# Second attention of an early-fusion network: the order of GpSimd's reciprocal roots and additions in one loop

## The chip, the cores and the metric

The kernel runs on one core of one Trainium2 chip. The time is that of the device, in microseconds (us), from the start of the one launch to its end. Each core has a matrix engine (TensorE, PE in the profile, with its weight loads as PEld), a vector engine (VectorE, DVE), a scalar engine (ScalarE, ACT), GpSimd (POOL) and a queue that issues transfers (SyncE, SP). Each engine works through its own list of instructions in order; semaphores are what one engine waits for on another.

## The reference, cut to what matters

The network has four levels. Each level adds an attention and then a feed-forward layer to `h` (16 batches of 192 tokens, 192 values each), and each of the eight layers works on normed rows of `h`:

```python
h = h + L0_attn(layernorm(h)); h = h + L0_ffn(layernorm(h))
h = h + L1_attn(layernorm(h)); h = h + L1_ffn(layernorm(h))
...

def _L1_attn_ref(x, Wqkv, Wproj, bproj, s_q, s_k, s_v, s_attn, s_after):
    qkv = x @ Wqkv.T                      # 12 heads of 16
    q = fake_quant(q, s_q, -4, 3) * scale; k, v likewise
    attn = fake_quant((q @ k.T) / N, s_attn, 0, 7)     # no softmax
    out = fake_quant(attn @ v, s_after, -4, 3)
    return out @ Wproj.T + bproj
```

The change lies in the second attention, `L1_attn`. The layer behind it is a mixture of 16 experts, whose router needs the rows of `h + L1_attn(...)` normed once more and multiplied by a router matrix; that is done in the same loop. Both norms need `1 / sqrt(variance + eps)` of each row, which is called the root here.

## The kernel before, in words

The program is a row of stages. `attention1` is the stage of the second attention; it stands behind the first mixture of experts and ahead of the routing of the second. It goes over the 16 batches. A batch is 192 rows of `h`, held as two halves of 96 partitions, so a `[96, 384]` tile is a batch's `h`.

The five engines each have a loop over `n`, written out pass by pass, in which the steps of several batches are interleaved: in pass `n` the scores of batch `n` are made, while batch `n+1` is turned and projected, batch `n+2` is collected and its norm taken, and batch `n-1` is projected out. What ties the loops together are the semaphores in `S`.

A batch's way through the loops, with the lines of the profile:

- VectorE: `collect_part` (L1545) adds the weighted expert answers to `h`. `spread_of(0, n)` (L1556, L1559, L1561) takes mean and variance of the incoming rows and signals `var0`. `norm_in` (L1570) waits for `root0` and writes `rows`. This is done for batch `n+2` in pass `n`, with `spread_in(n + 2)` behind `take_scores(n, 3)` and `norm_in(n + 2)` ahead of `take_scores(n, 5)`.
- TensorE: `turn_in` transposes `rows` (L207, `t_bank`), `queries` and `keys` (L1330) and `values` (L927, `t_bank`) project them in f32; `scores` (L1356) and `weigh` (L1369) are small bf16 matmuls; `project_out` (L927, `b_bank<-a_wp,a_o`) makes the attention's output. `turn_normed` (L207, `b_bank`) and `route_scores` (L927, `b_bank<-a_router`) serve the router.
- ScalarE copies and scales what TensorE leaves in PSUM (L1446, L1453, L1460, L1476), and writes the second norm's rows `rows2` (`norm_out`, L1485).
- VectorE clips to the quantized range (L1538, L1603), adds the projected output to `h` (`add`, L1613), takes its mean and variance with `spread_of(1, n)` (`var1`), and, once `root1` is there, the shift of the second norm (`shift_of`, L1581).
- GpSimd does four things: `add_bias(n)` (L1302) adds the projection's bias to `h` once the rows of batch `n` are normed; `grow(n)` (L1307) adds `rows2` to `h` once ScalarE wrote them; `root_of(0, n)` and `root_of(1, n)` (L1289) raise the variance to the power -0.5 for the incoming and for the finished rows. It issues no transfers in this stage.

SyncE brings the expert answers of batches ahead (waits for `collected`) and stores the finished normed rows (waits for `rows2`).

The order of each engine's list is written by hand. No planner and no priorities are in it: GpSimd takes the next step only when the one before it has had its semaphore.

Of the kernel before, what the change touches and what calls it, by code (L numbers as in the profile page):

```python
# [21 lines left out]
B, N, D = 16, 192, 192  # L22
# [1186 lines left out]
def attention1(k, weights, answers, wts, logits, normed, E):  # L1209
# [8 lines left out]
    with ExitStack() as ctx:  # L1218
# [41 lines left out]
        @block.sync  # L1260
        def _(sp):
            def bring(m):
                if m >= AHEAD:
                    sp.wait_ge(S["collected"], m - AHEAD + 1)
                for r in range(2):
                    sp.dma_start(got[m % AHEAD][:, r], answers[r * T + m * N:r * T + m * N + N].rearrange("(t p) d -> p t d", p=H2)
                                 ).then_inc(got_in[m % AHEAD], 16)

            def store(n):
                to = normed[n * N:(n + 1) * N].rearrange("(t p) d -> p t d", p=H2)  # L1270
                sp.wait_ge(S["rows2"], n + 1)
                sp.dma_start(to[:, :, 0:D], rows2[n % KEPT][:]).then_inc(kept[n % KEPT], 16)
                sp.dma_start(to[:, :, D:WIDE], rows2[n % KEPT][:, :, 128:D]).then_inc(kept[n % KEPT], 16)

            for m in range(6):
                bring(m)
            for n in range(B + 1):
                if n + 6 < B:
                    bring(n + 6)
                if n >= 1:  # L1280
                    store(n - 1)
            for u in range(KEPT):
                sp.wait_ge(kept[u], 32 * (B // KEPT))

        @block.gpsimd
        def _(pool):
            def root_of(r, n):
                pool.wait_ge(S[f"var{r}"], n + 1)
                nc.gpsimd.tensor_tensor(root[r][:], var[r][:], half[:], ALU.pow).then_inc(S[f"root{r}"], 1)  # L1289

            nc.gpsimd.memset(half[:], -0.5).then_inc(S["preset"], 1)
            for u in range(2):
                nc.gpsimd.memset(v[u][:], 0.0).then_inc(S["preset"], 1)
            pool.wait_ge(S["preset"], 3)
            root_of(0, 0)
            root_of(0, 1)
            pool.wait_ge(weights.loaded, weights.LOADED)

            def add_bias(n):
                pool.wait_ge(S["rows"], n + 1)  # L1300
                hb = h[:, 2 * n:2 * n + 2, :]
                nc.gpsimd.tensor_tensor(hb, hb, bias[:].unsqueeze(1).broadcast_to([H2, 2, D]), ALU.add).then_inc(S["biased"], 1)  # L1302

            def grow(n):
                pool.wait_ge(S["rows2"], n + 1)
                hb = h[:, 2 * n:2 * n + 2, :]
                nc.gpsimd.tensor_tensor(hb, hb, rows2[n % KEPT][:], ALU.add).then_inc(S["grown"], 1)  # L1307

            add_bias(0)
            for n in range(B + 2):  # L1310
                if n + 1 < B:
                    add_bias(n + 1)
                if 2 <= n:
                    grow(n - 2)
                if 1 <= n <= B:
                    root_of(1, n - 1)
                if n + 2 < B:
                    root_of(0, n + 2)

        @block.tensor  # L1320
        def _(pe):
# [1816 lines left out]
```

## Time and profile before

| | before |
|---|---|
| runs, median (lowest to highest) | 2682.95 us (2680.21 to 2687.97), 3 runs |
| profiled execution, its own time | 2685.28 us |
| its span in the trace | 2683.2 us |
| TensorE busy | 2387.4 us, 89% of the span |
| VectorE, ScalarE, GpSimd busy | 49%, 32%, 18% of the span |
| mean granted TensorE clock | 0.898 |
| GpSimd in this stage, first and last root | 602.9 and 873.4 us from the span's start |

The profile's times count from the span's start. The stage of the change takes some 280 of the 2683 us. The granted clock is the share of full TensorE speed (2.4 GHz) in a stretch: 1.00 and 0.50 are the two levels, and a value between them is a stretch that has some of both. "Idle before, with a releaser" is the time in which an engine had nothing to do and what ended it. Matmul ends are modelled.

### The profile page before, as it was taken

The page shows a single profiled execution, that of the slowest core. Times are in us where ns is not written, and L with a number is a line of the kernel's source. Part 1 is how long each engine was busy: PE and PEld are TensorE (multiplying, and loading weights), DVE is VectorE, ACT ScalarE, POOL GpSimd, SP SyncE. Part 2 cuts the span into 40 slices and gives each one's busy share as a digit, 9 for nine tenths or more (in the row PEclk, how much of TensorE's full clock was granted, in tenths as well). Part 3 has the DMA queues.
Part 4 walks back from the last instruction along what each step waited for, and adds up shares of the span by engine and source line. Part 5 has one row for each costly group of instructions (what it writes and reads, how often), then busy time and mean ns, then how long its engine had stood idle before and what let it go on. Part 6 is the DMA issues. An engine that isn't in the chain of part 4 may idle for free. (4 is left out here: it accounts for less than half of the span.)

```text
span 2683.2 us, 52183 instructions
## 1 busy us (share of the span) xinstructions
PE 2387.4 (89%) x17933; PEld 2084.2 (78%) x17933; DVE 1326.3 (49%) x3861; ACT 871.1 (32%) x2122; POOL 490.1 (18%) x583
## 2 busy tenths in 40 slices
PE   8968999988999489997999766999978899999997
PEld 8958999977777388887788665878747788888886
DVE  2663333326665711112688744555567456372644
ACT  2411222215555033332232212343444333343431
POOL 1233322222222334443122101000011000010100
PEclk8979999988655689998999856999989999999999
DMA  3134464511100368673000001000001452726355
GB/s 110 28 84 134 136 173 145 161 43 32 30 22 16 96 190 239 206 223 110 18 18 9 1 1 28 8 7 9 7 12 33 144 137 66 204 54 171 91 150 156
DMA packets 234529, 234.76 MB, mean 87 GB/s; under 512 B 29736, under 2 KB 214942, under 8 KB 234270
## 3 DMA queue, kind: packets, MB, share of 16 engines
q1 hardware_dynamic: 220638, 203.56, 27.4%
q0 software_dynamic: 11520, 27.54, 3.3%
q10 hardware_dynamic: 2240, 1.99, 0.3%
q8 instruction: 73, 1.20, 0.2%
q14 instruction: 58, 0.48, 0.1%
HBM read 277.77 MB, written 35.45 MB: 117 GB/s over the span
## 5 line engine op out<-in xcount | busy, mean ns | idle before, releaser
L732 PE MATMUL f_pg<-f_vxT,f_w 128*128 128x128 f32 x2112 | 261.0, 278 | 3.1 <-DVE f_vxT L802 3.1
L732 PEld LDWEIGHTS f_pg<-f_vxT,f_w 128*128 128x128 f32 x2112 | 253.4, 194 | 7.2 <-DVE f_vxT L802 4.6
L744 PE MATMUL f_po<-f_wd,f_hid 128*128 128x192 f32 x1440 | 254.3, 326 | 1.2 <-DVE f_vout L828 0.7
L744 PEld LDWEIGHTS f_po<-f_wd,f_hid 128*128 128x128 f32 x1440 | 231.2, 190 | 2.0 <-issue 1.7
L705 POOL DMA_INDIRECT f_answers<-f_vout,f_to_row x120 | 118.8, 990 | 423.9 <-DVE f_vout L826 250.7
L813 DVE TENSOR_TENSOR f_hid<-f_silu,f_pg 128x128 f32<-128x128 f32 x336 | 81.9, 285 | 214.8 <-ACT f_silu L781 199.5
L781 ACT ACTIVATE f_silu<-f_pg 128x128 f32<-128x128 f32 x336 | 78.4, 277 | 293.0 <-PE f_pg L738 274.0
L786 ACT ACTIVATE f_hid<-f_pg,f_b 128x128 f32<-128x128 f32 x384 | 110.9, 370 | 192.8 <-issue 109.0
L802 DVE COPY f_vxT<-f_pt 128x256 f32<-128x256 f32 x120 | 50.6, 422 | 208.1 <-PE f_pt L724 206.0
L738 PE MATMUL f_pg<-f_vxT,f_wr 64*128 64x128 f32 x2112 | 151.3, 285 | 0.0
L1926 DVE TENSOR_REDUCE a_low<-a_s_bank 96x6 f32<-96x1152 f32 x64 | 86.6, 1354 | 116.2 <-PE a_s_bank L1781 115.8
L738 PEld LDWEIGHTS f_pg<-f_vxT,f_wr 64*128 64x128 f32 x2112 | 128.2, 189 | 14.7 <-issue 0.4
L2767 PE MATMUL s_bank<-s_w,s_arena 128*128 128x192 f32 x768 | 133.4, 330 | 4.8 <-DMA s_b<-s_b_of 4.8
L2587 POOL TENSOR_TENSOR s_small<-s_small,s_half 128x2 f32<-128x2 f32 x64 | 44.4, 694 | 508.4 <-DVE s_small L2914 508.4
L2767 PEld LDWEIGHTS s_bank<-s_w,s_arena 128*128 128x128 f32 x768 | 123.9, 190 | 15.2 <-issue 9.3
L2984 DVE TENSOR_TENSOR s_y<-s_bank,s_b 128x384 f32<-128x384 f32 x64 | 35.3, 557 | 201.5 <-PE s_bank L2767 173.0
L2861 ACT ACTIVATE s_arena<-s_bank,s_b 128x256 f32<-128x256 f32 x192 | 73.6, 482 | 165.9 <-PE s_bank L2753 165.9
L699 POOL DMA_INDIRECT f_vrows<-f_normed,f_from_row x120 | 117.1, 976 | 43.2 <-issue 35.6
L2671 PE MATMUL s_bank<-h,s_arena 96*128 96x192 f32 x512 | 99.3, 337 | 22.2 <-ACT s_arena L2830 21.5
L2694 PE MATMUL s_bank<-s_ys,s_combine 128*96 128x193 f32 x512 | 97.0, 339 | 15.8 <-DMA s_ys<-s_y 9.5
L2671 PEld LDWEIGHTS s_bank<-h,s_arena 96*128 96x128 f32 x512 | 83.2, 191 | 34.5 <-ACT s_arena L2830 34.0
L2813 ACT ACTIVATE s_arena<-s_bank,s_small 128x192 f32<-128x192 f32 x128 | 52.7, 417 | 168.0 <-DVE s_combine L2897 168.0
(398 smaller groups left out, 4889.7 us busy)
## 6 DMA issues: line engine op xcount, KB each, us to landing
f_wd<-in_L_ffn_W SPq DMA_DIRECT2D x64, 576.0 KB
f_wd<-in_L_ffn_WdT SPq DMA_DIRECT2D x56, 576.0 KB
f_w<-in_L_ffn_W SPq DMA_DIRECT2D x64, 384.0 KB
f_w<-in_L_ffn_WgT SPq DMA_DIRECT2D x56, 384.0 KB
f_w<-in_L_ffn_WuT SPq DMA_DIRECT2D x56, 384.0 KB
s_w<-in_w SPq DMA_DIRECT2D x64, 288.0 KB, 3.7
f_wr<-in_L_ffn_W SPq DMA_DIRECT2D x128, 96.0 KB
s_w<-in_w SPq DMA_DIRECT2D x64, 192.0 KB, 4.3
```

What stands on the lines that cost most here:

```text
L699: pool.indirect_dma_start(out=rows[n % 3][:], out_offset=None, in_=normed, in_offset=bass.IndirectOffsetOnAxis(ap=from_row[:, n:n + 1], ax ...
L705: pool.indirect_dma_start(out=answers, out_offset=bass.IndirectOffsetOnAxis(ap=to_row[:, n:n + 1], axis=0), in_=out[n % 3][:], in_offset=N ...
L732: pe.matmul(pg[j][:, a * ROWS:(a + 1) * ROWS], lift[a][r][:, j * 128:j * 128 + 128], xT[r][:, 0, :], start=(a == 0), stop=False, skip_grou ...
L738: last = pe.matmul(pg[i + s * HALF][:, a * ROWS:(a + 1) * ROWS], rest[a][r][of, i * 128:i * 128 + 128], xT[r][of, 1, :], start=False, stop ...
L744: last = pe.matmul(po[:, 0:D], hid[r][:, j, :], wd[r][:, j, :], start=(at == 0), stop=(at == FC - 1))
L781: nc.scalar.activation(silu[at % 2][:], pg[j][:, 0:ROWS], ACT.Silu).then_inc(gates, 1)
L786: nc.scalar.activation(hid[r][:, j, :], pg[j][:, 0:ROWS], ACT.Gelu, bias=bias[:, ds(e, 1), j:j + 1].rearrange("p o n -> p (o n)")).then_in ...
L813: nc.vector.tensor_tensor(hid[r][:, j, :], silu[at % 2][:], pg[j][:, ROWS:2 * ROWS], ALU.mult).then_inc(hidden, 1)
L1926: nc.vector.tensor_reduce(low[:, :, EACH * c:EACH * c + EACH, DH].rearrange("p t e -> p e t"), s_bank[0:H2, :, 0:2 * N].rearrange("p e (t ...
L2671: last = pe.matmul(split(2 + b % 2, D)[:, c, :], disp[b % 2][:, t, c * 128:c * 128 + 128], h[:, 2 * b + t, :], start=(t == 0), stop=(t == 1))
L2694: last = pe.matmul(split(6 + b % 2, XA, H2)[:, t, :], weights_of(g)[:, c, t * H2:t * H2 + H2], ys[g % FETCHED][:, c, :], start=(c == 0), s ...
L2767: last = pe.matmul(split(6 + s, D)[:, f, :], hid[2 * p + s][:, c, f * 128:f * 128 + 128], w2[2 * p + s][:, c, :], start=(c == 0), stop=(c ...
```

## The change

In GpSimd's loop of `attention1` the root of the incoming rows of batch `n + 2` is taken ahead of the addition of normed rows of batch `n - 2` and ahead of the root of the finished rows of batch `n - 1`. It stood behind both. The addition of the bias stays first in the pass. Nothing else is touched.

```diff
             for n in range(B + 2):
                 if n + 1 < B:
                     add_bias(n + 1)
+                if n + 2 < B:
+                    root_of(0, n + 2)
                 if 2 <= n:
                     grow(n - 2)
                 if 1 <= n <= B:
                     root_of(1, n - 1)
-                if n + 2 < B:
-                    root_of(0, n + 2)
```

## Rows read from the trace of the kernel before

**Rows 1.** The page: TensorE's granted clock in 40 slices, in tenths.

```profile
PEclk8979999988655689998999856999989999999999
```

**Rows 2.** Waits, 603 to 885 us: total, times, longest.

```profile
DVE a_rows L1570 <- POOL a_root L1289: 20.9, 14, 1.5
...
PE a_t_bank L207 <- DVE a_rows L1570: 16.2, 8, 2.5
```

**Rows 3.** Timeline of a pass: start, duration, engine, line, idle before.

```profile
729.25 0.17 DVE L1561 TENSOR_SCALAR a_var<-a_mv 96x2 f32<-96x2 f32 x1
...
730.78 0.99 POOL L1307 TENSOR_TENSOR h<-h,a_rows 96x384 f32<-96x384 f32 x1 [10.12 <-ACT a_rows L1485]
...
731.54 0.61 DVE L1613 SCALAR_TENSOR_TENSOR h<-a_b_bank,a_s,h 96x384 f32<-96x384 f32 x1 [1.32 <-PE a_b_bank L927]
...
734.16 0.17 DVE L1561 TENSOR_SCALAR a_var<-a_mv 96x2 f32<-96x2 f32 x1
...
734.26 0.36 PE L1356 MATMUL a_s_bank<-a_qs,a_ks 32*96 32x192 bf16 x4
...
734.41 1.36 POOL L1289 TENSOR_TENSOR a_root<-a_var,a_half 96x2 f32<-96x2 f32 x2 [2.64 <-DVE a_var L1561]
...
735.88 0.67 DVE L1570 TENSOR_SCALAR a_rows<-h,a_mv,a_root 96x192 f32<-96x192 f32 x2 [1.55 <-POOL a_root L1289]
...
736.60 0.54 PE L207 MATMUL a_t_bank<-ident,a_rows 96*96 96x96 f32 x4 [1.97 <-DVE a_rows L1570]
736.62 1.53 POOL L1302 TENSOR_TENSOR h<-h,a_bias 96x384 f32<-96x384 f32 x1 [0.85 <-DVE a_rows L1570]
...
738.20 2.85 PE L1330 MATMUL a_p_bank<-a_xT,a_wqk 96*96 96x192 f32 x8
```

**Rows 4.** Timeline of the pass before it.

```profile
712.83 0.99 POOL L1307 TENSOR_TENSOR h<-h,a_rows 96x384 f32<-96x384 f32 x1 [8.81 <-ACT a_rows L1485]
...
718.39 0.67 DVE L1570 TENSOR_SCALAR a_rows<-h,a_mv,a_root 96x192 f32<-96x192 f32 x2 [1.55 <-POOL a_root L1289]
...
719.41 0.87 PE L207 MATMUL a_t_bank<-ident,a_rows 96*96 96x96 f32 x4
...
726.34 2.88 PE L1330 MATMUL a_p_bank<-a_xT,a_wqk 96*96 96x192 f32 x8
```

**Rows 5.** GpSimd's addition at the first, a middle and the last of 13 starts.

```profile
646.32 0.99 POOL L1307 TENSOR_TENSOR h<-h,a_rows 96x384 f32<-96x384 f32 x1 [9.59 <-ACT a_rows L1485]
...
746.99 0.99 POOL L1307 TENSOR_TENSOR h<-h,a_rows 96x384 f32<-96x384 f32 x1 [8.83 <-ACT a_rows L1485]
...
849.42 0.99 POOL L1307 TENSOR_TENSOR h<-h,a_rows 96x384 f32<-96x384 f32 x1 [8.84 <-ACT a_rows L1485]
```

**Rows 6.** Stretches: length, TensorE busy (instructions), granted clock, DMA share, GB/s.

```profile
731.00:732.00 1.00, 1.00 (x12) 0.96 0.39 101
...
737.00:738.00 1.00, 1.00 (x13) 0.96 0.00 0
...
765.00:766.00 1.00, 1.00 (x11) 0.89 0.25 62
```

**Rows 7.** Stretches: busy of PE, PEld, DVE, ACT, POOL, then the granted clock.

```profile
712.00:730.00 18.00, 18.00 (x98) 13.46 (x97) 10.51 (x31) 9.17 (x15) 3.88 (x4) 0.50 0.11 29
730.00:746.00 16.00, 14.03 (x97) 10.90 (x96) 10.24 (x30) 8.74 (x15) 3.88 (x4) 0.71 0.13 32
...
646.00:850.00 204.00, 190.22 (x1156) 145.30 (x1154) 122.80 (x351) 108.51 (x169) 46.92 (x49) 0.62 0.10 24
```

**Rows 8.** VectorE's shift of the second norm: shortest, median, longest ns.

```profile
L1581 DVE SCALAR_TENSOR_TENSOR a_shift<-a_mv,a_root x16: 149/972/975, 635.8 to 874.2; 96x2 f32<-96x2 f32 x16
```

**Rows 9.** Timeline near the stage's start, where the granted clock is 1.00.

```profile
623.03 0.36 PE L1356 MATMUL a_s_bank<-a_qs,a_ks 32*96 32x192 bf16 x4
...
624.92 1.47 PE L1330 MATMUL a_p_bank<-a_xT,a_wqk 96*96 96x192 f32 x8
...
632.35 0.36 PE L1356 MATMUL a_s_bank<-a_qs,a_ks 32*96 32x192 bf16 x4
```

## The prediction, made before the changed kernel ran

> **What bounds the kernel now.** I read the page first. TensorE is the busiest engine, and its granted clock dips in the middle of the first half of the span, in slices 11 to 14 [rows 1]; a slice is 67 us, so that dip, 671 to 939 us, is most of the stage of the second attention and the routing behind it. The waits of this stage came next [rows 2]: VectorE's norm of the incoming rows waits 14 times on GpSimd's root, 20.9 us in all, and TensorE's transposes of those rows wait 8 times on that norm, 16.2 us in all. 14 waits of VectorE but 8 of TensorE: in the other passes the stall is hidden. To see which, I read two successive passes in the timeline.
>
> In the first of them [rows 4] VectorE waits 1.55 us as well, yet its rows are ready at 719.06 and TensorE turns them at 719.41 with no idle time: TensorE is the bound, busy 18.00 us of 18.00 at half clock [rows 7]. In the second [rows 3], where TensorE is busy 14.03 of 16 us [rows 7], the granted clock is full from 731 to 738 us [rows 6]. TensorE comes through its list faster, stands 1.97 us for the rows, and turns them at 736.60. The stretch of full clock ends at 738, and the next begins at 765, so it comes in one pass of two here. GpSimd's addition marks the passes: 712.83, 730.78, 746.99 [rows 3 to 5]. So a pass all at half clock takes 17.95 us, one with a stretch of full clock 16.21, and the twelve passes from GpSimd's addition at 646.32 to that at 849.42 [rows 5] took 203.1 us, 16.9 each.
>
> **The change, part by part.** It adds and removes no instruction; 14 roots of the incoming rows move ahead of 12 additions and of 13 roots of the finished rows. No transfer is issued by GpSimd in the loop, and SyncE waits for nothing that GpSimd signals, so no queue but GpSimd's is reordered.
>
> *The moved root.* Its variance is ready at 729.42 (729.25 + 0.17) [rows 3]. GpSimd then has 10.12 us of idle time behind it and starts its addition only at 730.78. A root takes 0.68 us (two in 1.36) [rows 3]. After the change it runs from about 729.5 to 730.2, in time that was idle, 4 us before anyone asks for it. Cost: nothing; if the cover were gone, 0.7 us of the addition, for which nobody in the loop waits soon (ScalarE needs it four batches later).
>
> *What queues behind the new wait.* The addition waits for ScalarE's rows until 730.78, and the root of the finished rows needs its variance at 734.33 (734.16 + 0.17) [rows 3]. Both come later than 730.2, by 0.6 and 4.1 us. In this pass neither is held up.
>
> *The stall that goes.* VectorE's norm, in its place in VectorE's list, can start right after the finished rows' variance, at 734.33 and not at 735.88: 1.55 us earlier, its whole wait [rows 3]. The rows are there at 735.0. TensorE's scores end at 734.62, so it idles 0.4 us and not 1.97. What is late next is that same chain of the output projection, VectorE's addition and variance; its last 0.4 us remain as a wait for the rows.
>
> *Term 1.* Passes at half clock: 0, since TensorE is full there [rows 4, 7]. The 8 waits of TensorE [rows 2]: 8 x 1.55 = 12.4 us.
>
> *Term 2.* The transposes, the router scores and the query projection behind them move 1.55 us forward while the full clock ends, as before, at 738 [rows 3, 6]. The queries' 8 matmuls took 2.85 us at half clock, 0.356 us each [rows 3]; at full clock the same 8 took 1.47, or 0.184 each [rows 9]. They would start near 736.7 and have 1.2 us of full clock, six or seven matmuls, which saves 6.5 x 0.17 = 1.1 us in each such pass. A pass with a stretch then takes 16.21 - 1.55 - 1.1 = 13.6 us.
>
> *Term 3.* The stretches of full clock begin at 731 and 765 [rows 6], the first at the end of the unbroken row of key projection and output projection, 726.34 to about 731.5, when VectorE's addition gets its input (the longest piece of f32 matmuls in a pass) [rows 3, 4]; 765 is two passes on, and the same piece of the pass between raised nothing. Which pass gets one thus depends on the length of the passes, and that changes from 16.21 to 13.6 us. What share gets one afterwards the trace can't show. Bounds: one in two as now, or every one. I take 3 of 4, since a pass that follows at 13.6 us lies about 2.6 us earlier against the old rhythm and the unbroken piece is 5.2 us long. Over the twelve passes: 9 x 13.6 + 3 x 17.95 = 176.3, against 203.1: 26.8 us. With one in two it is 6 x 13.6 + 6 x 17.95 = 189.3, a gain of 13.8; with every one 163.2, a gain of 39.9. These sums hold terms 1 and 2 for the twelve passes; the first of the 8 waits lies ahead of them and adds 1.5.
>
> *The sum:* 26.8 + 1.5 = 28.3 us. The profiled execution took 2685.28 us, 2.1 us of it outside its span; that gives 2657.0, and set against the median of the runs shown, 2682.95, which is 2.3 lower, 2654.7. I forecast 2655 us.
>
> *A rule that speaks against the change.* VectorE's tiny shift, which stands near GpSimd's bias addition of 736.62 in time [rows 3], takes 0.97 us in the median and 0.15 at the shortest [rows 8]. So GpSimd work can hold up VectorE by 0.8 us. The moved root now runs from 729.5, and VectorE then is idle 1.32 us for TensorE, until 731.54 [rows 3]: up to that much is hidden. The Trainium skill says that GpSimd's SBUF interfaces are "shared with VectorE", with contention for instructions that use two ports or two SBUF inputs ("GPSIMD Engine Reference", section 1). By it the sum would be the same where VectorE idles, and the trace agrees.
>
> **The rivals.**
>
> *Only the wait goes.* The stretches become rarer or end sooner, or the passes fall out of the good rhythm half the time: the gain is term 1 alone up to the one-in-two case, 8 to 20 us, 2663 to 2675. For it: the rhythm of the stretches is strict now. Against: nothing takes term 2 away if the stretch keeps its length.
>
> *The full clock stays.* Near the stage's start the clock is full through, and a pass took 632.35 - 623.03 = 9.3 us [rows 9]; it lacked the router's scores and second transposes (an estimate: three times the 0.54 us of the four transposes at 736.60 [rows 3]), so a full pass would take about 10.9. What the rows show before the fall at 738 is the 1.97 us hole [rows 3, 6]; with 0.4 us left, the fall may not come. Twelve passes of 10.9 save 72 us: 2611. If it holds in six and the rest are as forecast (176.3 / 12 = 14.7), it is 203.1 - 6 x 10.9 - 6 x 14.7 = 49.5. Against: what TensorE does in that place is mostly transposes and small bf16 matmuls, and in the pass from 712 to 730 such work, without a gap, leaves the clock at 0.50 [rows 7]. The Trainium skill has a rule for this: activity releases the throttle, the default is the throttled state ("TensorE: Matmul & The Clock Gate", part 1). By it this rival is the outcome; the trace agrees only in that the fall follows a hole.
>
> *The wait is replaced.* The addition or the finished rows' root is held up by the new place, or VectorE is bound by its own work: no gain. Against: VectorE was busy 10.24 us of 16 in such a pass [rows 7], and the new place leaves 0.6 us of room. 2677 to 2691.
>
> *Slower: the stretches vanish.* If the new rhythm keeps missing the unbroken piece, every pass is one of 17.95 us: 12 x 17.95 = 215.4 against 203.1, 12 us more, 2695. A pass with a stretch and term 1 alone takes 14.66; it decides where fewer than one pass in three has one (17.95 - 3.3 x share = 16.9).
>
> **How the numbers follow.** The forecast case, gains of 20 to 42 us: 0.50. Only the wait goes: 0.21. The full clock stays in half of the passes or more, over 42 us: 0.17. The wait is replaced: 0.07. Slower: 0.05. 0.3% is 8 us, about what a measurement of this kernel can tell from no change. Faster by more than that: 0.88; within: 0.07; slower: 0.05. The range goes from 2632 (forecast case and the nearer third of the full-clock case) to 2673 (term 1 less a little), and leaves out 2 in 10.
>
> **What would show it.** VectorE's norm no longer waits on GpSimd's root (20.9 us to under 2). GpSimd's root of the incoming rows stands alone, some 4 us ahead of the other. TensorE's wait for the rows falls from 16.2 us to under 6. Passes alternate between about 13.6 and 17.95 us, and the granted clock of 646 to 850 us, 0.62 now [rows 7], rises to 0.67 or so. The other stages stay as they are. The prediction is wrong if the passes with a stretch stay above 15 us (term 2), if stretches come in half of the passes or fewer (term 3), or if they last longer than before (full clock).

## The result

The changed kernel takes 2603.12 us in the median of 4 runs (2595.94 to 2616.23), against 2681.58 us for the kernel before (4 runs, 2671.69 to 2687.97): a ratio of 0.9716, 95% interval 0.9662 to 0.9770. I forecast 2655 us and a range of 2632 to 2673; the time lies below both. The rival "The full clock stays" is what happened. The profiled execution took 2616.23 us, with a span of 2614.0; it is the slowest of the four.

The page of the changed kernel, its granted clock in 40 slices of 65 us, beside [rows 1]:

```profile
PEclk8979999998795999997999657999989999999999
```

Slices 11 to 14 stood at 6, 5, 5 and 6 [rows 1]. Now the half clock of the stage shows as the 8 and the 7 of slices 10 and 11 (588 to 719 us), and slice 12 is at 9; the 5 of slice 13 begins at 784 us and is mostly the routing behind the stage. To find the stage's end in each trace I took stretches with the same number of TensorE instructions. First the kernel before, a view that stands in none of its rows yet (columns as in [rows 7]; the clock is the third number from the end):

```profile
0.00:600.00 600.00, 545.45 (x4610) 518.48 (x4611) 239.74 (x958) 135.51 (x501) 157.34 (x193) 0.94 0.39 112
600.00:880.00 280.00, 257.09 (x1637) 199.69 (x1636) 165.85 (x480) 144.37 (x224) 61.47 (x64) 0.65 0.11 28
880.00:2683.20 1803.20, 1584.82 (x11688) 1366.08 (x11688) 920.73 (x2423) 591.20 (x1397) 271.34 (x326) 0.92 0.32 89
```

Then the changed kernel, with two stretches inside its stage at the end:

```profile
0.00:600.00 600.00, 545.55 (x4612) 520.57 (x4613) 239.73 (x959) 135.45 (x501) 157.49 (x193) 0.94 0.39 112
600.00:805.00 205.00, 192.72 (x1635) 153.07 (x1633) 158.87 (x480) 139.96 (x224) 63.15 (x64) 0.86 0.14 37
805.00:2614.00 1809.00, 1589.10 (x11688) 1367.50 (x11688) 920.75 (x2423) 586.70 (x1397) 271.21 (x326) 0.92 0.32 88
...
646.00:688.00 42.00, 42.00 (x227) 31.45 (x227) 24.67 (x74) 21.75 (x34) 7.68 (x9) 0.50 0.09 24
688.00:780.00 92.00, 88.83 (x867) 70.59 (x866) 85.78 (x261) 77.29 (x126) 36.27 (x36) 1.00 0.14 37
```

The stage with the same 64 GpSimd instructions went from 280 to 205 us and its mean clock from 0.65 to 0.86. The rest of the program gave 6 us back in this pair of executions (1809.0 against 1803.2), which leaves the 69 us between the two spans. That rest varies by more than this: from the stage's last addition to the end of the span it is 1794 us in the shortest and 1816 in the longest of the fourteen traces of this document, over the same code. So I give the length of the stage's passes beside the times below. Inside the stage there are now two regimes, and neither is the alternation that I forecast: a few passes at half clock, then full clock for 92 us on end.

The waits of the changed kernel from 603 to 885 us, beside [rows 2]:

```profile
DVE a_rows L1570 <- POOL a_root L1289: 0.8, 1, 0.8
...
PE a_t_bank L207 <- DVE a_rows L1570: 4.4, 11, 0.8
```

And its timeline in a pass at full clock, beside [rows 3]:

```profile
710.02 0.17 DVE L1561 TENSOR_SCALAR a_var<-a_mv 96x2 f32<-96x2 f32 x1
...
710.26 0.74 POOL L1289 TENSOR_TENSOR a_root<-a_var,a_half 96x2 f32<-96x2 f32 x1 [5.78 <-DVE a_var L1561]
...
710.98 1.32 POOL L1307 TENSOR_TENSOR h<-h,a_rows 96x384 f32<-96x384 f32 x1
...
712.29 0.17 DVE L1561 TENSOR_SCALAR a_var<-a_mv 96x2 f32<-96x2 f32 x1
...
712.37 0.67 DVE L1570 TENSOR_SCALAR a_rows<-h,a_mv,a_root 96x192 f32<-96x192 f32 x2
...
712.53 1.28 POOL L1289 TENSOR_TENSOR a_root<-a_var,a_half 96x2 f32<-96x2 f32 x1 [0.23 <-DVE a_var L1561]
...
713.09 0.54 PE L207 MATMUL a_t_bank<-ident,a_rows 96*96 96x96 f32 x4 [0.34 <-DVE a_rows L1570]
...
721.12 1.32 POOL L1307 TENSOR_TENSOR h<-h,a_rows 96x384 f32<-96x384 f32 x1
```

The root of the incoming rows now stands alone at 710.26, 2.1 us ahead of the norm at 712.37, which starts with no wait. TensorE's hole before its transposes (the idle time in front of them; this word from here on) is 0.34 us where it was 1.97 [rows 3]. From one addition to the next, 710.98 to 721.12, a pass takes 10.14 us. The fifteen passes from the first addition to the last take 12.2, 17.95, 17.95, 12.07, then eight of 9.16 to 10.24 (six of them 10.14), and 7.52 or less for the last three, which have less in them. With the two regimes read off, the same 17.95 us stands for half clock as before, so all of the gain is in how many passes run at full clock and in what such a pass takes.

### The profile page after: what moved, and what is told of

It reads as the page before. It is cut to its first block and busy times, and to the rows that moved or that the text cites. A ratio compares the mean times of both kernels' runs of the same rounds, so it can differ in the third digit from the quotient of the medians.

```text
span 2614.0 us, 52183 instructions
## 1 busy us (share of the span) xinstructions
PE 2327.4 (89%) x17933; PEld 2041.1 (78%) x17933; DVE 1319.4 (50%) x3861; ACT 862.1 (33%) x2122; POOL 491.8 (19%) x583
```

## The experiments

In each kernel the computation is the reference's. Some have *fillers* in front of TensorE's transposes of the incoming rows: matmuls of the identity with itself into unused columns of the same PSUM bank, work that nobody reads.

```diff
             def turn_in(n):
-                pe.wait_ge(S["rows"], n + 1)
                 pe.wait_ge(S["v8"], n)
+                if n >= 3:
+                    for _ in range(K):
+                        pe.matmul(t_bank[:, 384:512], k.ident[:], k.ident[:], start=True, stop=True)
+                pe.wait_ge(S["rows"], n + 1)
```

The fillers stand there from the fourth batch on. They fill the hole and, by the same act, give TensorE more work: what they show is that the hole with its lack of work matters, not which of the two. Ratios are to the kernel before on the same chip, whose median was 2683.1, 2681.8 and 2679.0 us in the three groups of runs; they are worked out from all runs, so they are not quite the quotients of the medians. What each of them did to the mean hole (TensorE's total wait for the rows by its count), to the twelve passes from GpSimd's first addition in the trace, and to the time:

| kernel | order of GpSimd's steps | mean hole, us | twelve passes, us | median us | ratio (95%) |
|---|---|---|---|---|---|
| before | addition, finished root, incoming root | 2.03 (8) | 203.1 | 2682 | 1 |
| half_hole | as after; norm waits for finished root | 1.30 (8) | 190.7 | 2676.57 | 0.9992 (0.9970 to 1.0014) |
| grow_first | addition, incoming, finished | 0.81 (10) | 167.5 | 2633.79 | 0.9818 (0.9778 to 0.9858) |
| grow_last | incoming, finished, addition | 0.38 (11) | 158.5 | 2636.32 | 0.9829 (0.9787 to 0.9872) |
| after | incoming, addition, finished | 0.40 (11) | 140.4 | 2603.12 | 0.9716 (0.9662 to 0.9770) |
| before_fill4 | before, 4 fillers | 1.43 (7) | 202.7 | 2673.31 | 0.9967 (0.9944 to 0.9990) |
| before_fill10 | before, 10 fillers | 0.37 (12) | 151.3 | 2616.11 | 0.9760 (0.9722 to 0.9797) |
| half_hole_fill4 | half_hole, 4 fillers | 0.40 (2) | 131.6 | 2600.11 | 0.9707 (0.9684 to 0.9729) |
| grow_first_fill4 | grow_first, 4 fillers | 0.2 (1) | 131.7 | 2593.76 | 0.9682 (0.9655 to 0.9708) |
| after_fill1 | after, 1 filler | 0.4 (1) | 120.8 | 2594.07 | 0.9664 (0.9645 to 0.9684) |

### Is it the clock? The old order with the hole filled

`before_fill10` is the kernel before with K = 10, nothing moved.

> The old order in GpSimd with ten filler matmuls ahead of the wait for the rows instead of four (2.7 us at full clock, 5.4 at half). With four, TensorE still stood 0.9 to 1.8 us for the rows and the clock still fell. Theory: the clock falls with the hole, and with the hole filled it stays at 1.00; a pass is then 10.14 + 1.55 for the root + 0.83 for VectorE's variance held up by GpSimd's addition = 12.5 us, and the kernel takes about 2683 - 13 x 4.4 + 5 = 2630 us. Rival, the clock follows something else: passes keep alternating, each low pass is 23 us long, and the kernel is slower than before, 2720 us or more.

Measured: 2616.11 us (2609.8 to 2623.56), ratio 0.9760. Its timeline in a pass, and a stretch of the stage:

```profile
706.34 0.99 POOL L1307 TENSOR_TENSOR h<-h,a_rows 96x384 f32<-96x384 f32 x1 [5.50 <-ACT a_rows L1488]
...
706.36 1.00 DVE L1564 TENSOR_SCALAR a_var<-a_mv 96x2 f32<-96x2 f32 x1
...
709.03 2.50 PE L1326 MATMUL a_t_bank<-ident 128*128 128x128 f32 x20
...
709.70 1.36 POOL L1289 TENSOR_TENSOR a_root<-a_var,a_half 96x2 f32<-96x2 f32 x2 [2.37 <-DVE a_var L1564]
...
711.17 0.67 DVE L1573 TENSOR_SCALAR a_rows<-h,a_mv,a_root 96x192 f32<-96x192 f32 x2 [1.55 <-POOL a_root L1289]
...
711.89 0.54 PE L207 MATMUL a_t_bank<-ident,a_rows 96*96 96x96 f32 x4 [0.36 <-DVE a_rows L1573]
```
```profile
646.00:790.00 144.00, 139.63 (x1322) 115.29 (x1319) 122.25 (x342) 98.25 (x158) 45.35 (x47) 1.00 0.13 32
```

VectorE still waits its whole 1.55 us; the wait that the change removes is untouched. Yet the clock is 1.00 through the stage and a pass takes 12.6 us, not 16.2 and 17.95. So some 66 of the change's 78 us can be had by keeping the clock alone. The timeline also gives the length of the hole without fillers: 2.50 + 0.36 = 2.86 us. It is longer than the 1.97 of [rows 3] since here VectorE's variance takes 1.00 us beside GpSimd's addition (706.34 and 706.36), where it took 0.17 at 729.25 [rows 3]. With 0.34 left in the changed kernel the difference is 2.5 us: 1.55 of the wait, 0.83 of that variance, and 0.1. That is the 12.60 - 10.14 = 2.46 us between the two full-clock passes.

Four fillers are too few for this order:

> The kernel before with the old order in GpSimd, plus filler: from the fourth batch on TensorE does four 128x128 f32 matmuls on the identity into unused columns of the bank of the transposes, ahead of its wait for the rows (about 1.0 us at full clock, 2.2 us at half clock). The stall of VectorE stays. Theory, the clock: the filler takes the place of the hole in TensorE's work, the granted clock stays at 1.00 for most passes, and a pass takes 10.14 + 1.55 = 11.7 us: 13 passes of about 5 us less, near 2620 us. Rival, the path: the stall is still on it and filler is only more work: no gain, or 10 us more, 2680 to 2695.

2673.31 us (10 runs, 2654.88 to 2686.22), ratio 0.9967 (0.9944 to 0.9990). TensorE in it, two passes:

```profile
766.72 1.16 PE L1326 MATMUL a_t_bank<-ident 128*128 128x128 f32 x8
...
768.76 0.54 PE L207 MATMUL a_t_bank<-ident,a_rows 96*96 96x96 f32 x4 [0.88 <-DVE a_rows L1573]
...
781.45 0.53 PE L207 MATMUL a_t_bank<-ident,a_rows 96*96 96x96 f32 x4 [1.79 <-DVE a_rows L1573]
```

Holes of 0.9 to 1.8 us remained, the passes still went between 12 and 19.8 us, and at half clock, where TensorE has no hole, the fillers are plain cost: 19.8 us a pass for 17.95. It missed what the clock theory expected of it, because I had taken the hole from [rows 3], where the clock is full for 7 us only; before_fill10 was built for the 2.86 us.

### One hole, one pass

`fill1_one_old` is `after_fill1` with the old order in pass 6 alone; `one_old` the changed kernel with it in pass 9 alone.

```diff
-                if n + 2 < B:
+                if n + 2 < B and n != 6:
                     root_of(0, n + 2)
...
                 if 1 <= n <= B:
                     root_of(1, n - 1)
+                if n == 6:
+                    root_of(0, n + 2)
```

> The kernel with one filler matmul, in which all passes ran at full clock, but with the old order of the two roots in pass 6 alone. Theory, the clock as a switch: the one longer hole takes the clock to 0.50 in that pass and the kernel from 2594 to 2602 to 2615 us; the profile has one to three passes of 12 to 18 us there. Rival, each pass pays its own stall: that pass is 1.5 us longer, the granted clock stays 1.00, 2595 or 2596 us.

TensorE around that pass, and stretches up to it, through it and behind it:

```profile
689.08 0.53 PE L207 MATMUL a_t_bank<-ident,a_rows 96*96 96x96 f32 x4 [2.37 <-DVE a_rows L1575]
```
```profile
646.00:689.00 43.00, 40.70 (x394) 32.27 (x392) 39.98 (x122) 35.16 (x57) 16.35 (x17) 1.00 0.20 50
690.00:700.00 10.00, 10.00 (x50) 8.26 (x51) 6.72 (x19) 5.11 (x9) 1.47 (x3) 0.50 0.01 2
701.00:760.00 59.00, 58.98 (x573) 46.83 (x573) 56.44 (x173) 49.81 (x81) 22.61 (x22) 1.00 0.14 36
```

A single hole of 2.37 us in a stage otherwise at full clock, and the clock falls behind it, stays at 0.50 for 10 us with TensorE busy throughout, and comes back. The three passes around it take 9.16, 16.39 and 12.13 us, 7.3 more than three of 10.13; the medians differ by 6.7 (2600.80 against 2594.07, ratio 0.9698, 0.9664 to 0.9732; the intervals overlap, and 2600.80 lies just below the range that I expected, so it is the trace that carries this). So one hole costs its own 2.4 us and about 5 more at half clock. The same in the changed kernel without the filler:

> The changed kernel, but in pass 9 alone GpSimd keeps the old order (the root of the incoming rows last). Theory, the clock as a switch: at full clock the pass takes 10.14 us; the one hole of about 1.9 us in TensorE takes the granted clock to 0.50, and it stays there for the rest of that pass and for one to three passes of 17.95 us. Cost against the changed kernel 8 to 25 us, and passes 1 to 8 as they were. Rival, each pass pays its own stall: the pass with the old order is 1.55 us longer, the clock stays at 1.00 in the passes behind it, and the kernel is 1.5 us slower than the changed one, 2605 us or so, which can't be told from it.

2596.15 us (2582.97 to 2615.27), ratio 0.9665 (0.9637 to 0.9693): not slower than the changed kernel, so the expected loss isn't in the times. What one hole costs is less than what changes from one execution to the next: the traces of the changed kernel and of its repetition (`after_again`, below) differ by a whole half-clock pass early in the stage, 140.4 against 147.7 us for the twelve passes, and the rest of the program by up to 20 us. In its trace the hole is there, and the fall with it (147.7 us for the twelve passes):

```profile
736.68 0.54 PE L207 MATMUL a_t_bank<-ident,a_rows 96*96 96x96 f32 x4 [2.79 <-DVE a_rows L1572]
```
```profile
690.00:737.00 47.00, 42.85 (x426) 33.72 (x424) 43.08 (x130) 37.89 (x61) 17.54 (x19) 1.00 0.21 54
738.00:747.00 9.00, 9.00 (x46) 7.30 (x46) 6.32 (x19) 4.44 (x8) 1.00 (x2) 0.50 0.00 0
```

### Which part of the order matters

`half_hole` has the changed order, and VectorE's norm waits for the finished root too (`dve.wait_ge(S["root1"], n)` ahead of `norm_in(n + 2)`), so that half of the old wait comes back.

> The changed kernel, GpSimd's new order kept, but VectorE waits for the root of the finished rows ahead of its norm of the incoming rows, as it need not. It puts back one root's time, 0.75 us, of the 1.55. Theory, the hole in TensorE's work decides on the clock: the hole grows from 0.34 to about 1.1 us, as large as with the addition first, and the kernel takes 2620 to 2645 us, with the clock falling every second or third pass. Rival, only the length of the path counts: 13 x 0.75 = 10 us more than the changed kernel at the most, 2605 to 2613, with the clock no lower than there.

2676.57 us (10 runs, 2667.72 to 2687.90), ratio 0.9992. The norm waits 0.81 us and not 1.55, and little or nothing is left of the gain: the interval allows 8 us at most. Both my expectations, 2620 to 2645 and 2605 to 2613, were far too low. Its timeline and a stretch:

```profile
647.64 0.54 PE L207 MATMUL a_t_bank<-ident,a_rows 96*96 96x96 f32 x4 [1.24 <-DVE a_rows L1570]
```
```profile
646.00:850.00 204.00, 195.08 (x1219) 147.60 (x1218) 127.52 (x363) 114.61 (x178) 48.94 (x49) 0.61 0.10 25
```

Here passes of 14.76 and of 17.96 us come in no fixed order, six of the one and five of the other. From 656 us on the full clock comes in stretches of 6.8 us, as before (there from 731.1 to 737.9 by [rows 6]); here one begins and one ends in these windows of 1 us, at about 721.7 and 728.6:

```profile
721.00:722.00 1.00, 1.00 (x5) 0.63 0.00 0
728.00:729.00 1.00, 1.00 (x10) 0.78 0.00 0
```

The hole is 0.73 us shorter than the 1.97 of before, and in a stretch of unchanged length that counts twice, once as the wait and once as 0.73 us more work at full clock: 16.21 - 1.46 = 14.75. So terms 1 and 2 of the prediction do describe a pass in this regime. That 14.76 is also near its 14.66, a pass with the whole wait gone and nothing more, is chance, since only half of the wait is gone here. With the hole filled by four fillers the same order is fast:

> The kernel with half of the stall put back (VectorE waits for the root of the finished rows), which took 2677 us, plus four filler matmuls ahead of the wait for the rows (1.0 us at full clock), as long as its hole of 1.24 us. Theory, the clock made the 70 us: with the hole filled all passes stay at full clock, 10.14 + 0.81 = 10.95 us each, 2600 to 2612 us. Rival, the stall itself costs that much: it stays at 2677 or above.

2600.11 us (2595.50 to 2604.49), ratio 0.9707. Every pass takes 11.05 us at a clock of 1.00:

```profile
646.00:780.00 134.00, 131.83 (x1274) 105.39 (x1273) 118.52 (x356) 106.84 (x173) 49.12 (x46) 1.00 0.13 35
```

11.05 is 10.14 and the 0.81 us of VectorE's wait, plus 0.1. The other half of the old wait thus costs 0.9 us a pass at full clock, and the clock that falls over it 76 us in all (2676.57 against 2600.11, or 190.7 against 131.6 in the twelve passes).

`grow_first` moves the incoming root ahead of the finished root alone, and leaves the addition in front of both.

```diff
                 if 2 <= n:
                     grow(n - 2)
+                if n + 2 < B:
+                    root_of(0, n + 2)
                 if 1 <= n <= B:
                     root_of(1, n - 1)
-                if n + 2 < B:
-                    root_of(0, n + 2)
```

> GpSimd's addition of the normed rows first, then the root of the incoming rows, then the root of the finished rows: the move past the finished rows' root alone. Theory: only being ahead of the finished rows' root takes the stall away, since the addition ends before the variance of the finished rows is ready. The same time as the changed kernel, 2595 to 2617 us, with passes of 10.14 us at full clock. Rival: the addition counts too, because it now stands ahead of the root whenever ScalarE's rows come late; then passes grow by up to 0.7 us, and the clock falls more often: 2625 us or more.

2633.79 us (2619.98 to 2642.20), ratio 0.9818. VectorE's norm doesn't wait in the loop, and still 31 us of the 78 are missing. The timeline shows where from:

```profile
638.85 0.99 POOL L1307 TENSOR_TENSOR h<-h,a_rows 96x384 f32<-96x384 f32 x1 [5.53 <-ACT a_rows L1485]
638.87 1.00 DVE L1561 TENSOR_SCALAR a_var<-a_mv 96x2 f32<-96x2 f32 x1
...
642.77 0.54 PE L207 MATMUL a_t_bank<-ident,a_rows 96*96 96x96 f32 x4 [1.16 <-DVE a_rows L1570]
```

When it waits only for ScalarE's rows, the addition starts 0.02 us ahead of VectorE's variance of the incoming rows, and that small instruction takes 1.00 us for 0.17. VectorE is late by 0.83 us for the rest of the pass, and the hole is 1.16. In the changed order the addition stands behind the root, which waits for that very variance: the two can't meet.

This trace also has holes of both kinds at full clock, without fillers. After a half-clock stretch the addition is late and misses the variance, and the hole is 0.34 us; in the next pass they meet, and it is 1.16:

```profile
657.74 0.54 PE L207 MATMUL a_t_bank<-ident,a_rows 96*96 96x96 f32 x4 [0.34 <-DVE a_rows L1570]
...
668.71 0.54 PE L207 MATMUL a_t_bank<-ident,a_rows 96*96 96x96 f32 x4 [1.16 <-DVE a_rows L1570]
```
```profile
654.00:670.00 16.00, 14.50 (x149) 11.13 (x147) 14.56 (x42) 12.81 (x21) 6.89 (x8) 1.00 0.25 63
671.00:677.00 6.00, 6.00 (x35) 4.54 (x34) 4.89 (x15) 3.02 (x5) 0.00 (x0) 0.50 0.00 0
```

Four holes of 0.34 us are followed by no fall before the next hole, and each of the five of 1.16 to 1.26 us by a fall within 2.3 us. With four fillers:

> The kernel with GpSimd's addition first (2634 us) plus the same four filler matmuls; its hole was 1.16 us. Theory: full clock throughout, passes of 10.14 + 0.83 = 10.97 us, of which the 0.83 is VectorE's variance held up beside GpSimd's addition: 2600 to 2612 us. Rival, the addition first costs in another way: it stays near 2634.

2593.76 us (2585.56 to 2600.49), ratio 0.9682; 10.97 us a pass, that is 10.14 + 0.83. The pass is as expected, the time below the 2600 to 2612 that I gave it: behind the stage this trace has the shortest rest of all, 1794 us.

```profile
646.00:760.00 114.00, 113.15 (x1081) 90.91 (x1080) 110.22 (x312) 90.19 (x146) 37.83 (x40) 1.00 0.14 37
```

`grow_last` puts the addition behind both roots (the wait for ScalarE's rows of batch `n - 2` that the addition brought with it stands ahead of the finished root, as before).

> GpSimd's addition of the normed rows behind both roots; the root of the finished rows waits for ScalarE's rows instead, as its buffer demands. If the addition is harmless wherever it isn't beside VectorE's variance: 2590 to 2615 us and passes of 10.1 us at full clock. If it now holds up VectorE's shift or the norm's successors for longer: passes of 10.3 to 10.9 us, 2615 to 2640.

2636.32 us (2624.52 to 2642.33), ratio 0.9829. The hole at the transposes is as short as in the changed kernel, but the addition now runs into the bias addition, and both into VectorE's collecting:

```profile
659.09 1.36 POOL L1307 TENSOR_TENSOR h<-h,a_rows 96x384 f32<-96x384 f32 x1
660.41 1.38 POOL L1302 TENSOR_TENSOR h<-h,a_bias 96x384 f32<-96x384 f32 x1
...
660.96 1.37 DVE L1547 SCALAR_TENSOR_TENSOR h<-a_got,f_wts,h 96x192 f32<-96x192 f32 x2
...
664.68 1.54 PE L927 MATMUL a_b_bank<-a_wp,a_o 96*96 96x192 f32 x8 [0.42 <-DVE a_o L1540]
```

The collecting takes 1.37 us for 0.74, VectorE comes late with the attention's output, and TensorE gets a second hole of 0.42 us. In the trace the clock is at 0.50 from 672 to 679, from 696 to 703 and from 720 to 764 us. That the second hole is what lets it fall is my reading; no run fills that one. It is the case in which the size of the hole at the transposes says nothing: the mean is 0.38 us and the time that of `grow_first`.

### The version that does best

> The changed kernel plus one such 128x128 filler matmul in each pass ahead of the wait for the rows (0.25 us at full clock, inside a wait of 0.34). Theory, the clock: it costs nothing at full clock and makes the fall at 644 us less likely, which cost three passes of 17.95 instead of 10.14 us: 2580 to 2605 us. Rival: the three slow passes have another cause, and the time stays at 2596 to 2616 us or is up to 4 us above.

The changed kernel with K = 1: 2594.07 us (2586.22 to 2594.80), ratio 0.9664. The half-clock passes at 646 to 688 us are gone, and passes take 10.13 us from the first:

```profile
646.00:765.00 119.00, 118.86 (x1159) 94.46 (x1159) 112.19 (x345) 101.76 (x166) 47.26 (x46) 1.00 0.15 39
```

> The changed kernel plus two filler matmuls per pass (0.5 us at full clock; the wait there is 0.34). Theory: all passes at full clock, each up to 0.2 us longer than 10.14, so 2590 to 2600 us, as with one filler or 2 us above, and less spread than the changed kernel. Rival: more filler costs more than it gives, 2600 or above.

K = 2: 2585.72 us (5 runs, 2581.51 to 2598.92), ratio 0.9664 (0.9638 to 0.9690), passes of 10.21 us, 121.6 us for the twelve. Beside it the changed kernel once more:

> The changed kernel once more, unaltered, for a comparison beside the one with two filler matmuls: 2595 to 2617 us, median near 2603. With the clock as the cause it varies by one to three slow passes of 8 us from run to run.

2602.83 us (6 runs, 2588.49 to 2616.16), ratio 0.9714 (0.9683 to 0.9745), as in the first comparison. One or two fillers thus bring the medians 9 to 17 us further down; the intervals of 0.9664 and 0.9714 touch, so a gain of half a per cent is likely and not certain. The twelve passes, 121 and 122 us against 140 and 148, say the same, for one trace each. The spread that I expected to shrink with two fillers is 17 us for 28. Both beat the kernel before and, in their medians, the changed one.

## Why the prediction was wrong

**What bounds the kernel now: right.** TensorE at half clock is full, and a half-clock pass takes 17.95 us in every kernel without fillers. The stall of 1.55 us is hidden there.

**The moved root: right.** It runs in GpSimd's idle time (5.78 us ahead of it at 710.26), and the norm's 14 waits of 20.9 us became one of 0.8. The finished root isn't held up either: it stands idle for 0.23 us and starts at 712.53, 0.07 us behind its variance (712.29 + 0.17).

**"Cost: nothing" for the addition: right in sign, with a gain missed.** At full clock the addition is held up by the root, against what I wrote of a half-clock pass, by about a microsecond (710.98, right behind the root of 710.26); nobody waits for it. I looked only for what that place could cost. In the trace of before it stood at 730.78, clear of VectorE's variance at 729.25 [rows 3], with the end of the pass before at half clock. At full clock the two coincide, and being moved behind the root is worth 0.83 us a pass (`grow_first_fill4` against `after_fill1`; in the medians of these two it doesn't show), and between `grow_first` and the changed kernel, with the clock, 31 us.

**The stall that goes, with "its last 0.4 us remain": right.** Where there is a hole it is 0.34 to 0.44 us, but for the first, of 0.82.

**Term 1: right in mechanism, small in weight.** 1.55 us a pass is what VectorE gains. At full clock that, with the 0.83, is 2.46 us a pass, about 30 us in twelve.

**Terms 2 and 3, the step that failed.** Both take it that full clock still comes in short stretches, that term 2's end "as before, at 738", and that only the share of passes with one changes, 3 of 4. What the runs showed in its place: the stretch had ended because of the hole. With a hole of 0.34 us instead of 2 the full clock held for 92 us on end. Where a stretch begins the prediction read rightly: the full clock of the changed kernel comes back at 688.8 us, beside the addition of 688.77, as it came at 731.1 beside that of 730.78. Twelve passes from the first addition took 140.4 us in the changed kernel, where the prediction had 176.3 and before had 203.1. Of these 62.7 us the forecast had 26.8; the first addition comes 5.7 us sooner (640.67 against 646.32), and the last three passes gain 6.9.

**The rival "The full clock stays": right, and weighed too low at 0.17.** It gave 2611 us, with full-clock passes of 10.9; they take 10.14. That 2611 lies so near is in part luck: it has twelve full-clock passes, 72 us, where the trace has some at half clock and 62.7 us, and the 12.6 us outside them aren't in it. My reason against it was that the same work without a gap leaves the clock at 0.50 [rows 7]. That is true, and it still stands in the changed kernel (42.00 us busy of 42.00 at 0.50), but it tells what doesn't raise the clock, and I used it for what doesn't keep it. Of the latter the trace of before had one witness, the fall at 738 behind the hole of 1.97 us [rows 3, 6]. The Trainium skill's rule that activity releases the throttle ("TensorE: Matmul & The Clock Gate", part 1) named this outcome; the fillers, which are nothing but activity, agree with it by 66 us, while the 42 busy us at 0.50 don't follow from it.

**"Slower: the stretches vanish" and "The wait is replaced": neither came.** VectorE isn't replaced as a bound yet, but it is near: busy 85.78 of 92 us at full clock, against 88.83 for TensorE.

**What stays open.** Whether the empty time itself or the work missing in it lets the clock fall: the fillers change both. The mean hole orders before, `half_hole`, `grow_first` and after, but `grow_last` stands outside that order with two small holes. And the changed kernel's own fall at 644 us comes behind a hole of 0.36 us, as short as those that later do no harm. What stands ahead of it and of no later one is a hole of 0.82 us one pass back:

```profile
632.62 0.54 PE L207 MATMUL a_t_bank<-ident,a_rows 96*96 96x96 f32 x4 [0.82 <-DVE a_rows L1570]
642.77 0.54 PE L207 MATMUL a_t_bank<-ident,a_rows 96*96 96x96 f32 x4 [0.36 <-DVE a_rows L1570]
```

The same pair, 0.81 or 0.82 and then 0.35 or 0.36 us, followed by a fall within 3 us, is in four traces without fillers: the changed kernel, `after_again`, `one_old` and `grow_last`. One filler leaves 0.40 us of the first and nothing of the second, and the fall is gone. Whether the first hole is what counts no run shows: none changes it alone. Nor is it shown why the changed kernel's times spread over 20 us or more. The number of half-clock passes has a part in it, but the rest of the program varies as much, and with two fillers the times still spread over 17 us.

## What to carry to other kernels

Where the granted clock changes within a stage, price a stall in two currencies: its own length, and the passes at half clock behind it; here a wait of 1.55 us a pass cost about 2.5 us a pass directly (with what it coincided with) and the clock of the whole stage besides. A mean clock near 0.6 with an idle hole ahead of each fall was the sign of it here, and matmuls that nobody reads, put in that hole, told in one run what the clock is worth, once there were enough of them: four, for a hole of 2.86 us, told nothing. Look for coincidences at the pace that the change will give, not at the one of the trace: at half clock GpSimd's addition and VectorE's variance missed each other by 1.4 us, at full clock and in the old order (`before_fill10`) they met in every pass.

## What the runs showed of the hardware

- One hole of 2.37 us in a stage at full clock is followed by 10 us at half clock with TensorE busy throughout; in `grow_first` holes of 1.16 to 1.26 us are each followed by a fall and holes of 0.34 are not; mean holes of 1.3 us (`half_hole`) and 2.0 us (before) go with a clock of 0.61 and 0.62 from 646 to 850 us; work without any hole can run at 0.50 for 42 us and rise then.
- Filler matmuls (128 x 128, f32) take 0.125 us a record at full clock in a row of twenty, two records each (20 in 2.50 us); the two records of a single one stand at 0.49 us together (`after_fill1`). At half clock four of them lengthen a pass by 1.84 us.
- Beside a GpSimd addition of 96 x 384, a VectorE instruction of 96 x 2 takes 1.00 us for 0.17, and one of 96 x 192, two inputs, about twice its time (1.37 us for two that otherwise take 0.74, `grow_last`). Not every instruction is hit: the two statistics beside the addition of 710.98 take their usual 0.61 and 0.24 us. GpSimd's addition takes 1.32 to 1.36 us there for 0.99, but 0.99 where the variance is the one that waits. The root of 712.53 stands at 1.28 us for 0.74, yet the next GpSimd instruction starts 0.75 us behind it, so that figure isn't its cost.
